# A scan kernel on one core: w formed with channels on partitions and turned once, dt kept doubled, D·u inside the even sum, four decay buffers

## What is computed

```python
xz = x @ in_proj_w.T
xc, z = jnp.split(xz, 2, axis=-1)
u  = causal_conv(xc, conv_w, 4 taps) + conv_b          # 512 channels
dt = jnp.clip(jax.nn.sigmoid(u @ dt_w.T + dt_b), 0.0001, 1.0)
A  = -jnp.exp(A_log);  Bm = u @ B_w.T;  Cm = u @ C_w.T   # 16 states
def step(state, inp):
    ut, dtt, bt, ct = inp
    dA = jnp.exp(jnp.clip(dtt[:, :, None] * A, -5.0, 5.0))
    dB = dtt[:, :, None] * bt[:, None, :] * ut[:, :, None]
    state = dA * state + dB + 1e-06
    y = jnp.sum(state * ct[:, None, :], axis=-1) + D * ut
    return (state, y)
...
y = y * jax.nn.silu(z)
return y @ out_w.T
```

## Time and profile before

| | |
|---|---|
| median of 3 runs | 1530.47 us (1528.64 to 1535.08) |
| the profiled execution | 1535.97 us, span 1534.2 us |
| mean granted clock of TensorE | 0.958 of full speed |
| busy: PE / DVE / ACT / POOL | 89% / 68% / 62% / 56% of the span |
| first to last scan | 495.6 to 1304.5 us, 512 scans of 1.21 us |

### The profile page before, as it was taken

One profiled execution on the slowest core, in us unless ns is written; L12 is line 12 of the kernel. 1 busy time (PEld: TensorE's weight loads), 2 busy tenths in 40 slices (PEclk: granted clock), 3 DMA queues, 4 the chain that ended last, 5 costly groups with the idle time before them and its releaser, 6 DMA issues.

```text
span 1534.2 us, 21845 instructions
## 1 busy us (share of the span) xinstructions
PE 1365.8 (89%) x6834; PEld 925.3 (60%) x6834; DVE 1044.8 (68%) x1565; ACT 958.6 (62%) x1781; POOL 851.6 (56%) x414
## 2 busy tenths in 40 slices
PE   5899887999997998998989989999899777749997
PEld 2566645999843555555655655556556444449996
DVE  6666535333241798999899989998998998552332
ACT  1222231434324899899998998989989998104342
POOL 1111002455200797888888878878878888024552
PEclk9999998999998999999999999999999999869999
DMA  9200024676420498797997987979969989526772
GB/s 301 69 27 27 28 83 137 192 215 208 121 72 15 102 220 181 171 219 174 207 217 167 212 207 173 219 165 207 218 150 209 227 201 229 160 97 191 211 215 82
DMA packets 100261, 250.35 MB, mean 163 GB/s; under 512 B 10873, under 2 KB 41726, under 8 KB 85824
## 3 DMA queue, kind: packets, MB, share of 16 engines
q0 software_dynamic: 23392, 133.98, 40.2%
q1 hardware_dynamic: 74688, 113.62, 24.7%
q10 hardware_dynamic: 2080, 1.47, 0.3%
HBM read 116.65 MB, written 18.88 MB: 88 GB/s over the span
## 4 chain that ended last, share of the span: by engine, by line
PE 61%; DVE 13%; ACT 12%; issue 9%; DMA 3%; POOL 1%; DVEq 0%; POOLq 0%; ACTq 0%
PE ps L1480 10%; PE ps L1224 10%; PE ps L1420 9%; PE ps L1429 8%; DVE arena L1130 4%; ACT arena L688 4%; ACT arena L698 4%; PE ps L1509 4%; PE ps L1249 4%; PE ps L1286 2%; PE ps L1380 2%; PE ps L1240 2%; PE ps L1341 2%; PE ps L1553 2%; DVE x L1130 1%
## 5 line engine op out<-in xcount | busy, mean ns | idle before, releaser
L453 POOL TENSOR_TENSOR arena<-arena 128x2048 f32<-128x2048 f32 x97 | 446.4, 4602 | 155.0 <-DVE arena L1130 148.5
L1130 DVE TENSOR_TENSOR_SCAN arena<-arena,ps 128x512 f32<-128x512 f32 x392 | 471.3, 1212 | 65.1 <-PE ps L1224 54.2
L1224 PEld LDWEIGHTS ps<-cst,arena 128*128 128x128 f32 x2428 | 300.9, 145 | 334.3 <-issue 213.5
L1224 PE MATMUL ps<-cst,arena 128*128 128x128 f32 x2428 | 374.9, 282 | 90.4 <-ACT arena L698 42.1
L688 ACT ACTIVATE arena<-arena,a_neg 128x512 f32<-128x512 f32 x512 | 366.2, 716 | 46.2 <-DVE arena L1130 34.0
L698 ACT ACTIVATE arena<-arena,m_bt 128x512 f32<-128x512 f32 x512 | 363.4, 710 | 0.9 <-PE ps L1224 0.9
L1480 PE MATMUL ps<-arena,tapw 128*128 128x512 f32 x512 | 261.0, 609 | 0.0
L422 POOL DMA_INDIRECT arena<-rows,arena x78 | 75.9, 973 | 190.1 <-DVE arena L986 166.9
L1006 DVE TENSOR_TENSOR arena<-ps,arena 128x256 f32<-128x256 f32 x78 | 33.2, 425 | 206.0 <-PE ps L1429 129.8
L1420 PEld LDWEIGHTS ps<-arena 128*128 128x128 f32 x1248 | 155.8, 197 | 3.8
L1130 DVE TENSOR_TENSOR_SCAN x<-arena,ps 128x512 f32<-128x512 f32 x120 | 143.6, 1210 | 20.4 <-PE ps L1224 18.0
(11 more groups left out here) (168 smaller groups left out, 1559.2 us busy)
## 6 DMA issues: line engine op xcount, KB each, us to landing
arena<-arena POOLq DMA_DIRECT2D x53, 1024.0 KB, 8.3
arena<-in_W SPq DMA_DIRECT2D x94, 512.0 KB, 8.2
x<-arena POOLq DMA_DIRECT2D x33, 1024.0 KB, 8.3
arena<-c_rows SPq DMA_DIRECT2D x128, 256.0 KB, 3.7
arena<-x POOLq DMA_DIRECT2D x16, 1024.0 KB, 8.8
rows<-x SPq DMA_DIRECT2D x16, 512.0 KB, 3.3
x<-x POOLq DMA_DIRECT2D x8, 1024.0 KB, 9.4
x<-residual SPq DMA_DIRECT2D x12, 512.0 KB, 5.7
```

Source lines behind the costliest of these rows:

```text
L453: g.tensor_tensor(h, h, m_c[i % RC].unsqueeze(1).to_broadcast([P, KI, SEQ]), ALU.mult)\
L1130: v.tensor_tensor_scan(out=h[:, k, :], data0=m_a[g % RA], data1=ps[SCAN_BANK[g % 3]][:, :], initial=0.0, op0=ALU.mult, op1=ALU.add).then_i ...
L1224: return t.transpose(bank, src[:, k * P:(k + 1) * P], ident)
```

## The change

What it does, piece by piece:

- u is no longer turned. `m_uturn` and `m_utevac` go. `m_weigh` now multiplies clipped dt and u where both lie with channels on partitions, in SBUF, into a new buffer `m_w`; PE turns that (`m_wturn`), and ACT copies the turned w to `m_wt` (`m_wtevac`).
- dt is kept as tanh + 1, twice the sigmoid: ACT's half-and-shift step goes, the clip becomes "add 1, not under 2e-4", A is scaled by -0.5, and the factor 0.5 goes into `m_weigh`.
- `m_skip` of the channel blocks 2 and 3 goes; their even `m_add` becomes one instruction that computes D·u plus the even chain sum from SBUF into the bank. Blocks 0 and 1 stay as they were.
- Four decay buffers instead of five, two slots ahead instead of three.
- Slots: `m_weigh` from 41, 45, 51, 56 to 39, 43, 49, 54; the turn stays at 40, 44, 50, 55; the copy by ACT, at 10, 18, 25, 35 until now, comes at 41, 46, 51, 56.

```diff
-RC, RA, AHEAD = 2, 5, 3
+RC, RA, AHEAD = 2, 4, 2
-UT_AT = (9, 17, 24, 34)
-DTT_AT = (40, 44, 50, 55)
+WTT_AT = (40, 44, 50, 55)
-UTC_AT = (10, 18, 25, 35)
+WTC_AT = (41, 46, 51, 56)
-SKIP_AT = (44, 50, 14, 15)
+SKIP_AT = (44, 50)
-WT_AT = (41, 45, 51, 56)
+W_AT = (39, 43, 49, 54)
...
-            def m_utevac(n, o):
+            def m_wtevac(n, o):
-                a.wait_ge(S("m_utr"), KI * n + o + 1)
+                a.wait_ge(S("m_dtr"), KI * n + o + 1)
...
-                a.activation(dt, dt, ACT.Tanh, bias=mvec[:, 1, o:o + 1], scale=0.5).then_inc(S("m_th"), 1)
-                a.wait_ge(S("m_th"), KI * n + o + 1)
-                a.activation(dt, dt, ACT.Copy, bias=0.5, scale=0.5).then_inc(S("m_dt0"), 1)
+                a.activation(dt, dt, ACT.Tanh, bias=mvec[:, 1, o:o + 1], scale=0.5).then_inc(S("m_dt0"), 1)
...
-                w = m_wt[n % 2][:, :, o * P:(o + 1) * P]
-                v.wait_ge(S("m_dtr"), KI * n + o + 1)
-                v.wait_ge(S("m_utc"), KI * n + o + 1)
-                v.tensor_tensor(w, ps[DTT_BANK[o]][:, :].rearrange("p (c d) -> p c d", c=CPB), w, ALU.mult)\
-                    .then_inc(S("m_wt"), 1)
+                v.wait_ge(S("m_dt1"), KI * n + o + 1)
+                if KI * n + o:
+                    v.wait_ge(S("m_dtr"), KI * n + o)
+                v.scalar_tensor_tensor(out=m_w, in0=m_dt[n % 2][:, o, :], scalar=0.5, in1=m_u[n % 2][:, o, :],
+                                       op0=ALU.mult, op1=ALU.mult).then_inc(S("m_w"), 1)
...
+                    v.wait_ge(S("m_y"), KI * b + k - 1)
+                    v.scalar_tensor_tensor(out=ps[4 + k % 2][:, :], in0=m_u[b % 2][:, k, :], scalar=mvec[:, 2, k:k + 1],
+                                           in1=m_h[H[NS * b]][:, k, :], op0=ALU.mult, op1=ALU.add).then_inc(S("m_add"), 1)
...
-            def m_uturn(n, o):
-                t.wait_ge(S("m_u"), KI * n + o + 1)
-                for c in range(CPB):
-                    last = t.transpose(ps[UT_BANK[o]][:, c * P:(c + 1) * P], m_u[n % 2][:, o, c * P:(c + 1) * P], ident)
-                last.then_inc(S("m_utr"), 1)
...
-            def m_dturn(n, o):
-                t.wait_ge(S("m_dt1"), KI * n + o + 1)
+            def m_wturn(n, o):
+                t.wait_ge(S("m_w"), KI * n + o + 1)
```

More of the change, by code:

```diff
@@ L260, in build @@
         m_a = [s.take(SEQ) for _ in range(RA)]
+        m_w = s.take(SEQ)
         m_h = [s.take(KI * SEQ).rearrange("p (k t) -> p k t", k=KI) for _ in range(5)]
@@ L589, in feed @@
                     a.wait_ge(S("m_aexp"), 1)
-                    a.activation(a_neg[:, :, :], a_neg[:, :, :], ACT.Copy, scale=-1.0).then_inc(S("m_aexp"), 1)
+                    a.activation(a_neg[:, :, :], a_neg[:, :, :], ACT.Copy, scale=-0.5).then_inc(S("m_aexp"), 1)
                     a.activation(mvec[:, 1, :], mvec[:, 1, :], ACT.Copy, scale=0.5).then_inc(S("m_aexp"), 1)
@@ L660, in m_bchi @@
                 a.activation(m_bc[0:2 * NS, :], ps[BC_BANK][0:2 * NS, :], ACT.Copy).then_inc(S("m_bchi"), 1)
-            def m_utevac(n, o):
-                a.wait_ge(S("m_utr"), KI * n + o + 1)
+            def m_wtevac(n, o):
+                a.wait_ge(S("m_dtr"), KI * n + o + 1)
                 a.activation(m_wt[n % 2][:, :, o * P:(o + 1) * P],
-                             ps[UT_BANK[o]][:, :].rearrange("p (c d) -> p c d", c=CPB), ACT.Copy)\
-                    .then_inc(S("m_utc"), 1)
+                             ps[WTT_BANK[o]][:, :].rearrange("p (c d) -> p c d", c=CPB), ACT.Copy)\
+                    .then_inc(S("m_wt"), 1)
             def m_thevac(n, o):
@@ L704, in m_pre @@
                     m_uevac(n, UC_AT.index(q))
-                if q in UTC_AT:
-                    m_utevac(n, UTC_AT.index(q))
+                if q in WTC_AT:
+                    m_wtevac(n, WTC_AT.index(q))
                 if q == BCC_AT:
@@ L1041, in _ @@
             v.wait_ge(S("m_aexp"), 3)
-            link(v.tensor_scalar(far[:, :], a_neg[:, :, :].rearrange("p k s -> p (k s)"), -5.0, None, ALU.is_lt))
+            link(v.tensor_scalar(far[:, :], a_neg[:, :, :].rearrange("p k s -> p (k s)"), -2.5, None, ALU.is_lt))
             v.tensor_reduce(far_sum[:, :], far[:, :], AX.X, ALU.add).then_inc(S("weights"), 1)
@@ L1048, in m_clip @@
                 v.wait_ge(S("m_dt0"), KI * n + o + 1)
-                v.tensor_scalar(m_dt[n % 2][:, o, :], ps[DT_BANK[o]][:, :], 1e-4, 1.0, ALU.max, ALU.min).then_inc(S("m_dt1"), 1)
+                v.tensor_scalar(m_dt[n % 2][:, o, :], ps[DT_BANK[o]][:, :], 1.0, 2e-4, ALU.add, ALU.max).then_inc(S("m_dt1"), 1)
             def m_btcopy(n):
@@ L1113, in m_pre @@
                     m_btcopy(n)
-                if q in WT_AT:
-                    m_weigh(n, WT_AT.index(q))
+                if q in W_AT:
+                    m_weigh(n, W_AT.index(q))
             def m_scan(g, clip):
@@ L1182, in m_all @@
                             m_close(b - 1, q)
-                        if b < BATCH - 1 and q in SKIP_AT[0:2]:
+                        if b < BATCH - 1 and q in SKIP_AT:
                             m_skip(b, SKIP_AT.index(q))
@@ L1519, in m_bturn @@
                 last.then_inc(S("m_btr"), 1)
-            def m_dturn(n, o):
-                t.wait_ge(S("m_dt1"), KI * n + o + 1)
+            def m_wturn(n, o):
+                t.wait_ge(S("m_w"), KI * n + o + 1)
                 for c in range(CPB):
-                    last = t.transpose(ps[DTT_BANK[o]][:, c * P:(c + 1) * P], m_dt[n % 2][:, o, c * P:(c + 1) * P], ident)
+                    last = t.transpose(ps[WTT_BANK[o]][:, c * P:(c + 1) * P], m_w[:, c * P:(c + 1) * P], ident)
                 last.then_inc(S("m_dtr"), 1)
@@ L1583, in m_prep @@
                             m_dtmm(n, o, k)
-                    if q == DTT_AT[o]:
-                        m_dturn(n, o)
+                    if q == WTT_AT[o]:
+                        m_wturn(n, o)
                 if q == BT_AT:
```

28 lines of the change are left out of this document (11 added, 17 removed).

## The result

| | before | after |
|---|---|---|
| median of 4 runs each, same chip | 1530.62 us (1528.64 to 1535.08) | 1573.78 us (1570.84 to 1578.36) |
| ratio, 95% interval | | 1.0276 [1.0257, 1.0296] |
| span of the profiled execution | 1534.2 us | 1569.1 us |
| mean granted clock | 0.958 | 0.950 |
| DVE / POOL busy | 68% / 56% | 69% / 55% |

The change costs 43.2 us. The two profiled spans differ by only 34.9, since the execution of after happened to reach the layer's first convolution 6.3 us sooner (423.7 against 430.0), with the same code ahead of it. From that convolution to the end of the last scan it takes 916.5 us instead of 874.5: +42.0. Of that, batches 1 to 6 make 40.6, batch 7 2.6, batch 0 0.9, and the lead-in -2.0 (batches are numbered 0 to 7, so batch 2 is the third).

What follows compares the result with a forecast made beforehand. Binding engine by stretch of a batch: A PE, B DVE (closing the previous batch), C PE, D PE and DVE, E ACT. Batches 1 to 6 +28.8, batch 7 +2.1, lead-in -2.2, clock 4: +32.7 on 1530.5, 1563 us, range 1534 to 1590.

Steps and rivals of the forecast that it cites:

- Hold at slot 16: First new even add, two SBUF inputs, waits for POOL's product of state 3 to end: held 3.57, cost 3.42 us.
- Second add, blocks 0, 1 and 3: Add behind slot 17 and `m_weigh` behind slots 39, 43, 54: no cost; only block 3 held, 0.3 to 0.4 us.
- rival 2: POOL is first at slots 39 and 43: 4.4 us twice a batch, +62, about 1624 us; 8%.
- Hold at block 2: `m_weigh` behind slot 49 held by POOL's product of state 11: cost 1.65 us ahead of slot 50's scan.
- Skips and u turns: Two skips leave the closing of the previous batch, -1.28 us; two u turns leave the PE-bound stretch, -0.88.
- w's path: PE's turns wait for `m_weigh`: 0.29 us at slot 40, slot 48's scan 0.4 late, slot 50's 1.0 without hold.
- Half-and-shift and buffers: Dropping ACT's step (about 0.49 us) gains nothing in the ACT-bound stretch; four decay buffers change nothing in the steady state.
- Lead-in, batches 0 and 7: Before the first scan -2.2 us; batch 0, without closing, 0; batch 7, only its closing, +2.1.
- The sum without the clock: Batches 1 to 6 +4.8 us each, +28.8; with batches 0 and 7 and the time before the first scan, +28.7.
- The half clock: New PE stands at slots 20 and 50 slow its clock: 0 to 15.6 us over six batches, 4 taken.
- rival 3: Half clock at nearly every stand: +28.7 + 13, about 1572 us; 12%.
- The price of one stand: Each new PE stand, at slots 20 and 50, may cost 0 to 1.3 us through a lower clock.

Runs made afterwards that it cites:

- skips_back: Changed kernel with the skips of blocks 2 and 3 back behind slots 14 and 15, even adds reading PSUM and one SBUF tensor: 1541.6 us (1.0064 of before).
- add_moved: Changed kernel with the new even adds moved from slots 16 and 17 to 15 and 19, odd ones to 19 and 20: 1539.5 us (1.0044 of before).
- filled_short: Changed kernel plus unread PE products, 4 behind the input of slot 19 and 3 ahead of block 2's turn: 1558.6 us (1.0183 of before).
- dt_and_buffers: Kernel before with only dt kept doubled (no half-and-shift by ACT) and four decay buffers, two slots ahead: 1523.6 us (0.9958 of before).
- w_moved: Changed kernel with w of blocks 2 and 3 formed behind slots 51 and 55, turned at 52 and 56: 1547.1 us (1.0100 of before).
- both_moved: Changed kernel with new even adds behind slots 15 and 19 and w of blocks 2 and 3 behind 51 and 55: 1526.4 us (0.9964 of before).
- old_w: Kernel before with dt doubled, four buffers and joined even adds behind slots 15 and 19, w formed the old way: 1513.4 us (0.9873 of before).

## Why the prediction held, and which term was too small

The forecast was 1563 in a range of 1534 to 1590; 1573.8 came. The runs bear out its direction and its mechanism, the two holds; one term, the half clock, was mis-sized.

- *Hold at slot 16.* Worked out 3.57 long, 3.42 in cost; measured 4.14 for the add, that is 3.41 over its twin's 0.73, and 3.42 in the batch. All seven are alike. Right.
- *Second add, blocks 0, 1 and 3.* Nothing forecast; 0.73, 0.67, 0.67 and 0.83. Right, and rival 2 (POOL first) doesn't occur. That 0.17 us suffice is shown.
- *Hold at block 2.* Forecast about 2.4, measured 2.23 (2.42 in batch 0). Right.
- *Skips and u turns.* From the scan of slot 15 to that of 16 it is 1.13 us now instead of 1.77, and the same from 14 to 15: -1.28. -0.88 + 0.29 in C: from slot 23 to 41 the scans take 27.53 us in `skips_back` and `add_moved`, 28.10 with the old order, -0.57. Right. In the changed kernel itself the half clock of slot 18 hides that gain (28.13).
- *w's path.* Slot 48 was put 0.4 late, and 0.37 is what -0.57 to slot 41 and +0.94 from there make. Slots 48 to 55 then take 15.72 instead of 13.17 without half clock, +2.55, for a term of 2.25 there (0.6 of order and 1.65 of hold). Right within 0.3. Slots 56 to 63 give 0.47 back at full clock (12.11 in `filled_short`, 12.58 in the second batch of before), for which no term stood.
- *Half-and-shift and buffers.* Nothing, since a copy of the turned w replaces it in E. `dt_and_buffers`, which has no such copy, gains, as the rule asks. The two weren't run apart, so what each gives stays open.
- *Lead-in, batches 0 and 7.* -2.2, 0 and +2.1 forecast; -2.0, +0.9 and +2.6 measured.
- *The sum without the clock.* +4.8 a batch. The changed kernel's batch without half clock takes 105.65. The kernel before has no such batch, but put together from eighths at full clock (slots 0 to 7 of its third batch, 56 to 63 of its second, the rest alike in all) it takes 101.15: +4.5. Right within 0.3.
- *The half clock.* Here the step "I take 4, a quarter, since PE has slack in B" failed. It was for two new stands, at slots 20 and 50. Both are paid: 0.5 us behind the first and 1.2 behind the second, 10 us over six batches where I took 4 of 15.6. PE's slack in B doesn't cover a slow stretch: at slot 24, where B ends, DVE waits 0.50 us for PE in after (739.15 in the third batch), and in `filled_short` it doesn't. The half clock at the batch's end, which I took as unchanged, costs 1.8 us a batch in after; before, where batches 2 to 6 have it, it costs about 1.2 (the six batches average 102.3). So all half clock together grew from 1.2 to 3.6 a batch, 14 over six.

Why there is more of it at the batch's end isn't shown. It doesn't simply come of the holds: with one of the two gone some batches have none there (2 to 6 of `w_moved`, 2 to 4 of `add_moved`, by the clock of slots 0 to 7 and 56 to 63), and with both gone batches 2 to 5 of `both_moved` begin at half clock again.

The total of 14 is near the 13 of rival 3, which gave 1572 and had 12%; that it came so close is partly luck, since 4 of the 14 lie at the batch's end, which rival 3 didn't count. Batches 1 to 6 were to take 106 to 107 us and took 107.9 to 109.7. The price of one stand, 0 to 1.3 us from the earlier trace rows, held for the two new ones; the share of it that is paid was too small.

## What to carry to other kernels

Before you give a DVE instruction a second SBUF input, look at what POOL runs at that moment; if it reads SBUF, place the instruction so that it begins ahead of POOL's, and the same edit turns from a loss into a gain (here +32 us, the changed kernel against `skips_back`, or -10, `old_w` against `dt_and_buffers`; `add_moved` against `skips_back` is only 2 us less, within the spread of the runs). Price a new wait by the stands that it makes on PE too: in the changed kernel half clock costs 3.6 us a batch, 1.7 of it behind the two stands that the holds make, and the two holds themselves cost 5.0.

## What was not expected of the hardware

- Idle time of PE can be worth filling: 7 products a batch that nobody reads made the kernel 15 us faster. It takes room that is truly free; 23 made it 70 us slower, and 2 elsewhere gained nothing.
- The length of a stand doesn't decide alone. Behind 2.57 us at slot 49 the clock fell to 0.50 in every batch from 1 to 6 of after, and behind 2.58 us it stayed at 1.00 in batches 2 to 4 of `add_moved`; its stretches around the stand in the fourth:

```profile
874.10:877.50 3.40, 0.84 (x5) 0.36 (x3) 3.40 (x4) 2.24 (x4) 3.03 (x2) 1.00 1.00 208
877.50:880.90 3.40, 3.37 (x17) 2.23 (x18) 3.40 (x5) 2.26 (x4) 0.67 (x1) 1.00 0.86 171
```

  What decides it, no run here tells apart.
